# Preparing four weight tiles in two pairs inside a decoder layer: the query weights of the cross attention

## The reference

```python
x = layernorm(x + self_attention(x))      # 16 heads of 128, weights = 4-bit codes times block scales
x = layernorm(x + cross_attention(x))     # Q = x @ W_qkv[:512].T, scores against ctx (1024 x 512)
x = layernorm(x + feed_forward(x))        # silu(gate) * up, 2048 wide
# cross_attention: scores = coef * Q @ ctx.T; all but the 54 largest of a row are masked;
#                  softmax; out = att @ ctx; out @ W_o.T
```

## Time and profile before

| what | value |
|---|---|
| median of 3 runs | 929.99 us (929.85 to 930.69) |
| the profiled execution, its own time | 932.48 us |
| its span | 930.7 us |
| mean granted TensorE clock | 0.996 of full speed |
| busy: PE, DVE, ACT, POOL | 910.8, 589.2, 581.3, 498.3 us |
| quarters 114 to 122 (by the work on ACT) | about 461 to 493 us of the span |

### The profile page before, as it was taken

One profiled execution on the slowest core, in us unless ns is written; L12 is line 12 of the kernel. 1 busy time (PEld: TensorE's weight loads), 2 busy tenths in 40 slices (PEclk: granted clock), 3 DMA queues, 4 the chain that ended last, 5 costly groups with the idle time before them and its releaser, 6 DMA issues.

```text
span 930.7 us, 13237 instructions
## 1 busy us (share of the span) xinstructions
PE 910.8 (98%) x4440; PEld 748.9 (80%) x4440; DVE 589.2 (63%) x1058; ACT 581.3 (62%) x1153; POOL 498.3 (54%) x413
## 2 busy tenths in 40 slices
PE   8999999999999999999999999999999999999997
PEld 6788778888788887888778788898888888888885
DVE  4667866767757678576775799887698125411114
ACT  3757786777866779677886576543654635433333
POOL 3256661646715557566775467644674752354440
PEclk9999999999999999999999999999999999999999
DMA  6522220131310213221222213333433341343321
GB/s 204 151 78 90 71 91 16 30 89 59 92 29 29 78 40 105 57 75 49 77 68 91 69 46 91 91 103 82 127 108 103 102 125 34 123 126 92 90 80 45
DMA packets 46102, 76.97 MB, mean 83 GB/s; under 512 B 5584, under 2 KB 11216, under 8 KB 45776
## 3 DMA queue, kind: packets, MB, share of 16 engines
q1 hardware_dynamic: 45600, 75.68, 28.1%
q10 hardware_dynamic: 432, 0.39, 0.2%
HBM read 73.69 MB, written 2.36 MB: 82 GB/s over the span
## 4 chain that ended last, share of the span: by engine, by line
PE 45%; DVE 4%; ACT 2%; issue 1%; DVEq 0%; ACTq 0%
PE p L927 6%; PE p L928 6%; PE p L931 6%; PE p L941 3%; PE p L942 3%; PE p L943 3%; PE p L880 2%; PE p L881 2%; PE p L885 2%; PE p L792 1%; PE p L789 1%; PE p L790 1%; PE p L774 1%; PE p L775 1%; PE p L778 1%
## 5 line engine op out<-in xcount | busy, mean ns | idle before, releaser
L1548 DVE TENSOR_SCALAR_CACHE_REDUCE JK<-p,ssc 128x512 bf16<-128x512 f32 x112 | 83.7, 747 | 113.6 <-PE p L676 113.6
L2047 POOL TENSOR_TENSOR V<-RAW,V 128x512 fp32r<-128x512 f32 x64 | 81.5, 1295 | 126.1 <-ACT V L1112 126.1
L1055 ACT ACTIVATE PR<-p,nms,ssc 128x512 f32<-128x512 f32 x112 | 87.4, 781 | 57.8 <-DVE JK L1548 56.3
L2043 POOL TENSOR_TENSOR acc<-SX,acc 128x512 f32<-128x512 f32 x56 | 72.4, 1293 | 81.8 <-ACT SX L1092 51.7
L694 PE MATMUL p<-R 128*128 128x512 f32 x248 | 97.2, 392 | 0.8 <-DVE V L1541 0.8
L2047 POOL TENSOR_TENSOR C<-RAW,C 128x512 fp32r<-128x512 f32 x58 | 77.2, 1341 | 30.8 <-ACT C L1112 30.7
L1561 DVE TENSOR_TENSOR PT<-p,PT 128x512 fp32r<-128x512 f32 x128 | 87.5, 683 | 5.2 <-ACT PT L1074 5.1
L1870 DVE TENSOR_TENSOR SX<-p,SX 128x512 f32<-128x512 f32 x32 | 22.1, 689 | 100.1 <-PE p L931 90.2
L729 PEld LDWEIGHTS p<-ident,PR 128*128 128x128 f32 x512 | 62.4, 140 | 21.3 <-DVE PT L1561 6.6
L729 PE MATMUL p<-ident,PR 128*128 128x128 f32 x512 | 77.4, 273 | 1.0
L1074 ACT ACTIVATE PT<-p 128x512 fp32r<-128x512 f32 x128 | 75.7, 592 | 0.0
(11 more groups left out here) (249 smaller groups left out, 2723.0 us busy)
## 6 DMA issues: line engine op xcount, KB each, us to landing
RAW<-in_wg SPq DMA_DIRECT2D x32, 256.0 KB, 2.8
RAW<-in_wu SPq DMA_DIRECT2D x32, 256.0 KB, 2.6
RAW<-in_ctxn SPq DMA_DIRECT2D x32, 256.0 KB, 2.8
RAW<-in_wd SPq DMA_DIRECT2D x32, 256.0 KB, 2.8
RAW<-in_wq SPq DMA_DIRECT2D x19, 256.0 KB, 2.7
RAW<-in_wk SPq DMA_DIRECT2D x18, 256.0 KB, 2.8
RAW<-in_wv SPq DMA_DIRECT2D x16, 256.0 KB, 2.8
RAW<-in_wo SPq DMA_DIRECT2D x16, 256.0 KB, 5.0
```

Of the source, the lines that this page charges most:

```text
L1055: e.activation(PR[:, i % 2, :], P[i % 2][:, :], ACT.Exp, bias=nms[:, i % 4:i % 4 + 1], scale=ssc[:, 0:1] if HB[j][0] > 1 else SC, accum_ou ...
L1548: e.tensor_scalar(JK[:, :], P[i % 2][:, :], ssc[:, 1:2] if HB[i // 4][0] > 1 else -SC, None, ALU.mult, ALU.min, accum_out=nms[:, i % 4:i % ...
L2043: e.tensor_tensor(acc[:, r], scaled_at(4 * q + tt), acc[:, r], ALU.add).then_inc(*rows[r].up((q, 1)))
L2047: e.tensor_tensor(lo, RAW[:, slot[key], :], hi, ALU.subtract).then_inc(*c_lo.up(key))
```

## The change

Before, tile kt is prepared (high half on ACT, low half on POOL) at the end of quarters 114, 115, 118 and 119, the third and fourth quarters of j = 28 and 29. After, tiles 0 and 1 are prepared at the end of quarter 116 and tiles 2 and 3 at the end of quarter 120, the first quarters of j = 29 and 30. The call that loads the tiles is moved in the same way in SP's program. The tiles, the instructions and their number stay the same.

```diff
# sync (SP)
-                if j in (28, 29) and qt >= 2:
-                    kt = 2 * (j - 28) + qt - 2
-                    load_raw(("xw", 0, kt), xwq[:, kt])
+                if i in (116, 120):
+                    for kt in (0, 1) if i == 116 else (2, 3):
+                        load_raw(("xw", 0, kt), xwq[:, kt])
# scalar (ACT), and the same in gpsimd (POOL)
-                if j in (28, 29) and qt >= 2:
-                    conv_xw(0, 2 * (j - 28) + qt - 2)
+                if i in (116, 120):
+                    for kt in (0, 1) if i == 116 else (2, 3):
+                        conv_xw(0, kt)
```

## The result

The changed kernel takes 931.61 us (median of 20 runs, 930.64 to 933.88) against 930.04 us of the kernel before (20 runs, 927.88 to 931.01). The ratio is 1.002, with an interval of 1.0012 to 1.0027: slower by 1.1 to 2.5 us. The forecast was 932.0 us, 2.0 us over the time before.

The account below looks back on a forecast made before the run. PE, busy 98% of the span, was taken to bound the kernel. The sum, 0 + 0 - 0.07 given back at `ln_std` + 1.97 at the transposes, about +2.0 us, gave 932.0 us; 8-in-10 range 930.8 to 932.7.

Parts of the forecast that it names:

- Quarters 114 and 115, nothing: Conversions taken out there free ACT 1.04 us earlier and POOL 2 x 1.25 us; both slack, so no gain.
- Quarter 116, DVE 0.45 us late: ACT's two conversions delay DVE's qk_low(30, 1) by 0.3 us; POOL's add_bias(2) delays o_add(13, 2, 0) by another 0.2.
- Quarter 118, gain of 0.07: Without ACT's conversion, pt_high(119) is ready for attend(29) 0.07 us earlier; of PE's 0.42 us stop nearly nothing comes back.
- Quarter 119, `ln_std` waits for DVE: On ACT, ln_std waits for DVE's late statistics, so ACT reaches the exponential of quarter 122 0.35 us late.
- Quarter 120, `qk_low(31, 1)` 1.0 us late: Two ACT conversions ahead of qk_high(31, 1) delay DVE's qk_low(31, 1): 1.04 + 0.35 us, only 0.4 of it slack.
- The lockout, another 1.0 us: In quarters 120 to 122 POOL's conversion and add_bias(6) hold up DVE's two ln_apply; PE's transposes come 1.97 us late altogether.
- Loads, nothing: SP's four moved tile loads keep their order and land in time, 2.8 us after issue; no cost.
- ACT alone (+1.0): Rival for quarters 120 to 122: DVE and POOL don't disturb each other, only ACT delays; +1.0 us, 931.0; chance 0.2.
- The hidden pairs (-0.4): Rival: ACT's pairs cost nothing and PE's stop at 478.80 in quarter 118 goes; -0.4 us, 929.6; chance 0.1.
- POOL's queue in quarter 116: Rival: add_bias(2) there becomes the bound, making DVE, ln_std and everything behind later; +3 us, 933; chance 0.05.

Follow-up runs that it names:

- POOL's pair moved: Against the kernel before: tiles 0 and 1 converted in quarter 116 on ACT, in 117 on POOL behind its bias of row 2; 931.07 us, single run.
- the pair in quarter 120 alone: Against the changed kernel: tiles 0 and 1 back in quarters 114 and 115, tiles 2 and 3 still in 120; ratio to the kernel before 1.0012.
- the run with one tile: Against the kernel before: tile 2 in quarter 118 ahead of the exponential, tile 3 in 120 behind POOL's bias of row 6; 928.20 us, single run.
- the bias ahead: Against the changed kernel: POOL's bias of row 6 moved from quarter 121 into 120, before the conversions; ratio to the kernel before 1.0011.
- the pair in 116 alone: Against the changed kernel: tiles 2 and 3 back in quarters 118 and 119, tiles 0 and 1 still in 116; ratio to the kernel before 1.0003.
- the biases under the norm: Against the kernel before: one wait added on POOL, so its biases of rows 5 and 6 start only after DVE normalises row 1; ratio 1.0012.
- tiles 2 and 3 ahead of the exponential: Against the kernel before: tiles 2 and 3 both converted in quarter 118, on ACT before its exponential; tiles 0 and 1 unmoved; ratio 1.0002.

## Why the prediction held

The forecast of 2.0 us was made as a sum on the trace, and the trace shows 2.07 between the landmarks. The measured 1.6 us (1.1 to 2.5) agrees within its interval but can't confirm the second digit. That the terms are right is therefore read from the traces; the time alone could not tell this sum from one of 1.5 us.

*Quarters 114 and 115, nothing.* Right: the lead of the changed kernel's execution is 1.95 us at 70 us and 1.96 at the landmark in quarter 116, so nothing was won or lost between.

*Quarter 116, DVE 0.45 us late.* Right, and split as predicted. `qk_low(30, 1)` came 0.27 us late (471.07 - 467.94 = 3.13, before 472.76 - 469.90 = 2.86). `o_add(13, 2, 0)` came 0.49 us late (6.03 against 5.54), after POOL's bias that ended at 473.86. With POOL's pair moved, 0.21 us of this went.

*Quarter 118, gain of 0.07.* The time of `attend(29)` was right: 8.89 us after the landmark, 8.90 before, a gain of 0.01. What I had said to look for was wrong: its idle time is not unchanged but falls, on the weight load from 0.85 to 0.31 us and on PE from 0.42 to none that the profile shows, because PE arrives later. The idle time has moved ahead, to 0.39 us behind `qk_low(30, 1)` and 0.51 us (0.28 before) at the projection in quarter 120.

*Quarter 119, `ln_std` waits for DVE.* Right: 0.37 us of idle time at 480.82, released by the statistics. The exponential of 122 came at 16.04 us after the landmark; I had 15.93, before it was 15.58. The term was 0.46 and not 0.35: the statistics were 0.50 us late, and `ln_std` started 0.12 us after their end.

*Quarter 120, `qk_low(31, 1)` 1.0 us late.* Measured 18.56 against 17.46 before: 1.10, which is 0.46 from the exponential plus 1.04 for two conversions, less 0.40 of slack. The run with the pair in quarter 120 alone gives nearly the same slack (1.04 - 0.06 - 0.57 = 0.41), and the run with one tile shows the same wait of DVE for ACT with one conversion.

*The lockout, another 1.0 us.* Shown from both sides: taking the bias away gives back 0.97, and putting biases under the pair in the kernel before costs 0.48. In detail I was off: I had the first `ln_apply` wait for POOL's second conversion and the second for the bias. Only the second waited. The first got in between two instructions of POOL and held up the bias (1.53 us), the second ended 0.28 us after it, as around 610 us. The first took 0.54 us and the second 1.51. The end is the same, since POOL's bias sets it either way. The Trainium skill's rule on the shared ports (SBUF — State Buffer, § Who interferes with whom) is exclusion for a whole instruction. These runs agree with it except for about the last 0.2 us of POOL's profiled spans, under which an `ln_apply` began unhindered, and the sum by it, 2.0 to 2.2 us, agrees with the 2.07 of the trace.

*Loads, nothing.* Right: no stop of ACT for a query tile appears in the stretch.

Of the rivals, ACT alone (+1.0) is what the kernel with the bias ahead does, +1.10; it is a part of the cause, not the whole. The hidden pairs (-0.4) exist, but ahead of the exponential in quarter 118. POOL's queue in quarter 116 is a term of 0.2 us and no bound.

## What to carry to other kernels

An engine's free time must be looked up at the instruction behind which the work is put, not in the quarter as a whole: in quarter 120 PE is long busy, but ACT stood just behind two table loads with 0.4 us to spare, while two quarters earlier it waited 2 us for DVE. When work of POOL moves, look at what DVE does in the new place and at what POOL has queued behind: a pair of instructions that takes 1 us alone took 2. And for an effect of 0.2%, as here, compare stretches of traces between two landmarks that the edit does not touch; spans of single executions can point the wrong way.

## What the runs showed of the hardware

POOL's profiled end is later than its hold on DVE. An `ln_apply` started 0.21 us before the end of POOL's conversion and took its normal time. One that came earlier ended 0.28 us after POOL's end in the changed kernel (489.72 against 489.44) and around 610 us, and 0.29 us after it with the biases under the norm (its 1.05 us from 485.61, against 486.37). Since it takes 0.54 us by itself, it must have begun some 0.25 us before POOL's profiled end. Whether POOL lets go early or its end is recorded late, no run shows.

The other difference between the two spans sits at 600 us, far from the edit. There PE waits 2 us for DVE in both kernels. The timelines of PE, before and changed:

```profile
600.68 1.33 PE L863 MATMUL p<-ident,SX 128*128 128x128 f32 x8 [1.96 <-DVE SX L1632]
601.66 2.06 PE L904 MATMUL p<-WV,R 128*128 128x512 f32 x4
```

```profile
600.79 1.18 PE L863 MATMUL p<-ident,SX 128*128 128x128 f32 x8 [1.98 <-DVE SX L1633]
601.72 1.18 PE L904 MATMUL p<-WV,R 128*128 128x512 f32 x4
```

And the busy times of PE, its weight loads, DVE, ACT and POOL from 602 to 604 us, then the granted clock, before and changed:

```profile
602.00:604.00 2.00, 2.00 (x8) 1.62 (x7) 0.24 (x1) 1.68 (x4) 2.00 (x2) 0.50 0.00 0
```

```profile
602.00:604.00 2.00, 1.84 (x12) 1.46 (x10) 1.06 (x2) 1.79 (x4) 2.00 (x2) 1.00 0.00 0
```

After nearly the same idle time of PE (1.96 and 1.98 us) the clock was granted at half (1.2 GHz) in one execution and in full (2.4 GHz) in the other, which cost the kernel before 0.93 us there. Of the nine profiled executions three show a mean granted clock of 0.66 to 0.72 from 600 to 605 us (before, the pair in 116 alone, the bias ahead), the other six 1.00. It follows no edit, since the kernel before shows it too, nor the length of the idle time, which is 1.95 to 2.00 us in all nine. The stretch near the start is of the same kind: the granted clock falls to half there, within the first 20 us, in three of the nine (the kernel before; tiles 2 and 3 ahead of the exponential, mean 0.60 from 10 to 14 us; POOL's pair in 117, 0.81 there). The one at 600 us is of the size of the effects studied here; how much of the changed kernel's lead of 1.96 us comes from it is not shown.
